# Top-p attention on one core: eight strip segments and four rounds in the second step, with another estimate of the band's end

## The reference, cut to what matters

```python
def _top_p_attention(X, W1, W2, W3):
    q = X @ W1.T @ W2.T
    k = X @ W3.T
    probs = jax.nn.softmax(q @ k.T / TAU, axis=-1)          # 2048 x 2048
    idx = jnp.argsort(-probs, axis=-1)
    sp = jnp.take_along_axis(probs, idx, axis=-1)
    cs = jnp.cumsum(sp, axis=-1)
    keep_sorted = cs - sp < TOP_P                           # TOP_P = 0.9
    mask = jnp.zeros(probs.shape, dtype=bool).at[rows, idx].set(keep_sorted)
    A = probs * mask
    return A / jnp.maximum(A.sum(-1, keepdims=True), 1e-12)
...
for n in range(STEPS):                                      # STEPS = 2
    A = _top_p_attention(Xa, W1, W2, W3)
    Xf = R @ Xf
    Xa = A @ Xa
    Z = Z + Xf @ U1[n].T + Xa @ U2[n].T
```

## Time and profile before

| | |
|---|---|
| median of 3 runs | 858.69 us (857.1 to 860.33) |
| the profiled execution | 859.55 us, span 857.8 us |
| PE, DVE, ACT, POOL busy | 85%, 73%, 53%, 32% of the span |
| the second step's groups, 495.4 to 784.2 us | DVE busy 274.8 of 288.8 us, ACT 185.0, POOL 126.3 |
| HBM | 57 GB/s over the span |

### The profile page before, as it was taken

One profiled execution on the slowest core, in us unless ns is written; L12 is line 12 of the kernel. 1 busy time (PEld: TensorE's weight loads), 2 busy tenths in 40 slices (PEclk: granted clock), 3 DMA queues, 4 the chain that ended last, 5 costly groups with the idle time before them and its releaser, 6 DMA issues.

```text
span 857.8 us, 15889 instructions
## 1 busy us (share of the span) xinstructions
PE 725.4 (85%) x5287; PEld 550.3 (64%) x5294; DVE 626.7 (73%) x2265; ACT 450.7 (53%) x689; POOL 273.9 (32%) x585
## 2 busy tenths in 40 slices
PE   4799999849999688999999997968678697798893
PEld 2566766529998444777777676755446585787463
DVE  6336656715444468998981799999899999999757
ACT  2366476115555145655653582849687585722153
POOL 4310422555666201112100152142250667770000
PEclk9899999879999899999999998879979898989897
DMA  9999730186887300000000000000000002001001
GB/s 155 193 173 156 136 72 16 40 213 192 231 235 205 118 1 1 1 1 2 2 2 1 1 2 2 2 1 2 0 1 1 2 2 74 26 3 32 1 2 49
DMA packets 82186, 50.37 MB, mean 59 GB/s; under 512 B 42193, under 2 KB 78929, under 8 KB 82097
## 3 DMA queue, kind: packets, MB, share of 16 engines
q1 hardware_dynamic: 64304, 28.35, 15.0%
q0 software_dynamic: 11456, 14.62, 9.1%
q10 hardware_dynamic: 6336, 6.32, 3.1%
HBM read 39.69 MB, written 9.57 MB: 57 GB/s over the span
## 4 chain that ended last, share of the span: by engine, by line
DVE 37%; PE 16%; ACT 5%; issue 5%; DVEq 1%; POOLq 1%; POOL 0%; ACTq 0%
DVE big L1602 6%; DVE cand L1366 5%; DVE cand L1520 4%; PE bank L2145 3%; PE bank L2049 3%; DVE hacc L1515 2%; DVE rm L1360 2%; DVE cand L1541 2%; DVE top L1536 2%; DVE big L1591 2%; PE bank L2128 2%; PE bank L2329 2%; DVE big L1588 2%; PE bank L2342 1%; ACT UT L1861 1%
## 5 line engine op out<-in xcount | busy, mean ns | idle before, releaser
L2128 PE MATMUL bank<-ident,big 128*128 128x128 f32 x512 | 79.6, 304 | 28.4 <-DVEq L1625 19.1
L2128 PEld LDWEIGHTS bank<-ident,big 128*128 128x128 f32 x512 | 61.2, 153 | 54.4 <-DVEq L1625 21.0
L1875 ACT ACTIVATE big<-bank 128x512 f32<-128x512 f32 x128 | 70.4, 597 | 46.6 <-PE bank L2128 46.6
L2049 PE MATMUL bank<-kk,qq 64*128 64x512 f32 x256 | 76.0, 711 | 16.8 <-ACT big L1845 16.2
L2056 PEld LDWEIGHTS bank<-parts,adjT 128*128 128x128 bf16 x1536 | 86.9, 98 | 3.2 <-issue 2.8
L2056 PE MATMUL bank<-parts,adjT 128*128 128x128 bf16 x1536 | 88.2, 219 | 0.1
L1845 ACT ACTIVATE big<-bank,negm 128x2048 f32<-128x2048 f32 x32 | 62.7, 1958 | 48.7 <-DVE fsc L1652 38.4
L1602 DVE SCALAR_TENSOR_TENSOR big<-big,st 128x2048 f32<-128x2048 f32 x32 | 73.9, 2348 | 2.9 <-PE bank L2128 2.9
L572 DVE TENSOR_TENSOR big<-big,adjT 128x1024 f32<-128x1024 f32 x32 | 39.8, 1249 | 48.5 <-ACT big L731 30.8
L428 POOL DMA_INDIRECT ys_scratch<-big,parts x62 | 59.9, 967 | 38.7 <-ACT big L774 28.6
L858 PEld LDWEIGHTS bank<-xrows,big 128*128 128x128 f32 x512 | 62.2, 196 | 14.6 <-DVE big L572 9.7
(11 more groups left out here) (373 smaller groups left out, 1448.1 us busy)
## 6 DMA issues: line engine op xcount, KB each, us to landing
big<-in_L_ffn_w_dram SPq DMA_DIRECT2D x93, 128.0 KB
big<-in_adj_dram POOLq DMA_DIRECT2D x8, 512.0 KB, 9.1
big<-xs_scratch ACTq DMA_DIRECT2D x31, 132.0 KB
kk<-in_adj_dram POOLq DMA_DIRECT2D x4, 512.0 KB, 11.3
qq<-in_adj_dram POOLq DMA_DIRECT2D x4, 512.0 KB, 15.0
xs_scratch<-hacc SPq DMA_DIRECT2D x9, 132.0 KB
xs_scratch<-hacc ACTq DMA_DIRECT2D x8, 132.0 KB
res<-in_x_dram SPq DMA_DIRECT2D x4, 256.0 KB, 5.0
```

Source lines behind the costliest of these rows:

```text
L1875: nc.scalar.activation(MT[:, 4 * q:4 * q + 4, s * P:(s + 1) * P], bank[:, 5 + q % 2, :].rearrange("p (j i) -> p j i", j=4), ACT.Copy).then ...
L2049: nc.tensor.matmul(bank[:, c, :], qq[lo:lo + DA, (g * G + s) * P:(g * G + s + 1) * P], kk[lo:lo + DA, c * CH:(c + 1) * CH], start=True, st ...
L2128: mm = nc.tensor.transpose(bank[:, 5 + q % 2, j * P:(j + 1) * P], mk[:, s, jt * P:(jt + 1) * P], ident[:, :])
```

## The change

Only the second step of the second graph layer changes.

- Each row tile's candidates come from 8 segments of 256 columns instead of 16 of 128. A segment is no longer one run of columns: it is four strips of 64 columns that stand 256 columns apart, all in one half of the row.
- Four rounds instead of five, on 64 candidates instead of 128; the 32 largest values below the band's end are used instead of 40. The short operations behind the rounds get shorter with it.
- `after_first` and `after_second` use another formula with a term that goes like the reciprocal of the count of values above the threshold. `after_first` has 12 operations instead of 8, with four drains as before; `after_second` has 11 as before, with five drains instead of six.

```diff
-        NSEG = (8, 16)
-        ROUNDS = (4, 5)
+        NSEG = 8
+        ROUNDS = 4
+        STRIPS = 4
...
-        SLOPE = 0.7
-        REACH = 40.0
+        JUMP = (1.23, 9.05, 0.476)
+        STEP = (1.0 / 0.823, 32.84, 38.66, 1.663)
...
                         nc.gpsimd.tensor_scalar(B(B_Y, s), B(B_S1, s), float(N), 0.5 * 2.0 ** FIRST, ALU.add, ALU.mult)
+                        nc.gpsimd.tensor_scalar(B(B_C, s), B(B_S1, s), -0.5, 0.5 * N + JUMP[2], ALU.mult, ALU.add)
...
                     nc.gpsimd.tensor_tensor(B(B_B, s), B(B_Y, s), B(B_R1, s), ALU.subtract)
-                    nc.gpsimd.tensor_scalar(B(B_TG, s), BI(B_TG, s), 1.0 / SLOPE, None, ALU.mult)
+                    nc.gpsimd.tensor_scalar(BI(B_C, s), BI(B_C, s), -1.0, 2.0 * ONE, ALU.mult, ALU.add)
+                    nc.gpsimd.tensor_scalar(B(B_TG, s), BI(B_TG, s), 1.0, None, ALU.mult)
                     pool.drain()
-                    nc.gpsimd.tensor_scalar(B(B_U, s), BI(B_B, s), -1.0 / SLOPE, ONE + FIRST * OCTAVE, ALU.mult, ALU.add)
+                    nc.gpsimd.tensor_scalar(B(B_U, s), BI(B_B, s), -1.0, B(B_TG, s), ALU.mult, ALU.add)
+                    nc.gpsimd.tensor_scalar(B(B_C, s), B(B_C, s), JUMP[1], JUMP[0], ALU.mult, ALU.add)
+                    nc.gpsimd.tensor_scalar(B(B_W, s), B(B_TG, s), STEP[0], None, ALU.mult)
                     pool.drain()
-                    nc.gpsimd.tensor_tensor(B(B_U, s), B(B_U, s), B(B_TG, s), ALU.add)
+                    nc.gpsimd.tensor_scalar(B(B_U, s), B(B_U, s), B(B_C, s), ONE + FIRST * OCTAVE, ALU.mult, ALU.add)
                     pool.drain()
...
-                    R8 = 8 * ROUNDS[n]
-                    SEG = N // NSEG[n]
-                    cg = cand1 if n else cand[:, b, :, :]
+                    R8 = 8 * ROUNDS
+                    cg = cand[:, b, :, :]
...
-                            for j in range(NSEG[n]):
-                                vc = op(nc.vector.max(cg[:, s, 8 * j:8 * j + 8], lowg[:, j * SEG:(j + 1) * SEG]))
+                            strips = lowg.rearrange("p (h a j n) -> p h j a n", h=2, a=STRIPS, j=NSEG // 2)
+                            for j in range(NSEG):
+                                vc = op(nc.vector.max(cg[:, s, 8 * j:8 * j + 8],
+                                                      strips[:, j // (NSEG // 2), j % (NSEG // 2), :, :]))
...
-                    for r in range(ROUNDS[n]):
+                    for r in range(ROUNDS):
...
-                            w = op(nc.vector.tensor_scalar(cand2[:, s, 0:64], cg[:, s, 64:128], S1(V_, s), None,
+                            w = op(nc.vector.tensor_scalar(cand2[:, s, 0:32], cg[:, s, 32:64], S1(V_, s), None,
                                                            ALU.is_equal, ALU.add, accum_out=S1(MH, s)))
```

More of the change, by code:

```diff
@@ L1044, in tries @@
             return 4 + 8 * (g - 1) + 2 * (2 * k + s) if g else 2 * s + k
-        tv = sb("tv", [P, G, 8 * max(ROUNDS)])
+        tv = sb("tv", [P, G, 8 * ROUNDS])
         cand = sb("cand", [P, 2, G, 64])
-        cand1 = cand[:, :, :, :].rearrange("p b s n -> p (b s n)").rearrange("p (s n) -> p s n", s=G)
-        top = sb("top", [P, G, 8 * max(ROUNDS)])
-        cum = sb("cum", [P, G, 8 * max(ROUNDS)])
+        top = sb("top", [P, G, 8 * ROUNDS])
+        cum = sb("cum", [P, G, 8 * ROUNDS])
         rm8 = sb("rm8", [P, 8])
@@ L1055, in build @@
         (T_, TB, F_, GE, Q_, FH, V_, SM, LO, HI, THETA, EX, EM, MH, DH) = range(15)
-        bt = sb("bt", [P, 13, G])
-        (B_R1, B_S1, B_R2, B_S2, B_T2, B_TB, B_TB1, B_TG, B_Y, B_B, B_C, B_U, B_V) = range(13)
+        bt = sb("bt", [P, 14, G])
+        (B_R1, B_S1, B_R2, B_S2, B_T2, B_TB, B_TB1, B_TG, B_Y, B_B, B_C, B_U, B_V, B_W) = range(14)
         first = sb("first", [P, 1])
@@ L1061, in build @@
         iota8 = sb("iota8", [P, 8])
-        cand2 = sb("cand2", [P, G, 128])
+        cand2 = sb("cand2", [P, G, 64])
         fsc = sb("fsc", [P, 2, G])
@@ L1220, in after_second @@
                     if g:
-                        nc.gpsimd.tensor_scalar(B(B_C, s), B(B_S2, s), float(N), 0.5, ALU.add, ALU.mult)
+                        nc.gpsimd.tensor_scalar(B(B_Y, s), B(B_S2, s), float(N), 0.5, ALU.add, ALU.mult)
+                        nc.gpsimd.tensor_scalar(B(B_C, s), B(B_S2, s), -0.5, 0.5 * N + STEP[3], ALU.mult, ALU.add)
                     else:
                         pool.wait_ge(counted, 2 * s + 2)
-                        nc.gpsimd.tensor_scalar(B(B_C, s), B(B_S2, s), 1.0, None, ALU.mult)
@@ L1225, in after_second @@
-                    nc.gpsimd.tensor_tensor(B(B_TG, s), B(B_TG, s), B(B_V, s), ALU.add)
+                        nc.gpsimd.tensor_scalar(B(B_Y, s), B(B_S2, s), 1.0, None, ALU.mult)
+                        nc.gpsimd.tensor_scalar(B(B_C, s), B(B_S2, s), -1.0, N + STEP[3], ALU.mult, ALU.add)
+                    nc.gpsimd.tensor_tensor(B(B_TG, s), B(B_W, s), B(B_V, s), ALU.add)
                     pool.drain()
-                    nc.gpsimd.tensor_tensor(B(B_Y, s), B(B_C, s), B(B_T2, s), ALU.mult)
@@ L1228, in after_second @@
-                    nc.gpsimd.tensor_scalar(B(B_C, s), B(B_C, s), -1.0, N + 0.5, ALU.mult, ALU.add)
+                    nc.gpsimd.tensor_tensor(B(B_Y, s), B(B_Y, s), B(B_T2, s), ALU.mult)
+                    nc.gpsimd.tensor_scalar(BI(B_C, s), BI(B_C, s), -1.0, 2.0 * ONE, ALU.mult, ALU.add)
                     pool.drain()
                     nc.gpsimd.tensor_tensor(B(B_B, s), B(B_Y, s), B(B_R2, s), ALU.subtract)
-                    nc.gpsimd.tensor_scalar(BI(B_C, s), BI(B_C, s), -1.0, 2.0 * ONE, ALU.mult, ALU.add)
+                    nc.gpsimd.tensor_scalar(B(B_W, s), B(B_C, s), STEP[2] * OCTAVE, STEP[1] * OCTAVE, ALU.mult, ALU.add)
@@ L1232, in after_second @@
                     pool.drain()
-                    nc.gpsimd.tensor_scalar(B(B_U, s), BI(B_B, s), -1.0 / SLOPE, None, ALU.mult)
-                    nc.gpsimd.tensor_scalar(B(B_C, s), B(B_C, s), REACH * OCTAVE, None, ALU.mult)
+                    nc.gpsimd.tensor_scalar(B(B_U, s), BI(B_B, s), -STEP[0], B(B_TG, s), ALU.mult, ALU.add)
+                    nc.gpsimd.tensor_tensor(B(B_W, s), B(B_W, s), B(B_C, s), ALU.mult)
                     pool.drain()
-                    nc.gpsimd.tensor_tensor(B(B_TG, s), B(B_TG, s), B(B_C, s), ALU.add)
@@ L1237, in after_second @@
-                    pool.drain()
-                    nc.gpsimd.tensor_tensor(B(B_U, s), B(B_U, s), B(B_TG, s), ALU.add)
+                    nc.gpsimd.tensor_tensor(B(B_U, s), B(B_U, s), B(B_W, s), ALU.add)
                     pool.drain()
@@ L1536, in group @@
                             got[s] = op(nc.vector.max(top[:, s, 8 * r:8 * r + 8], cand2[:, s, :] if n and r else cg[:, s, :]))
-                        if r + 1 < ROUNDS[n]:
+                        if r + 1 < ROUNDS:
                             for s in range(G):
```

1 line of the change is left out of this document (added).

## The result

The changed kernel takes 850.48 us (median of 20 runs, 847.06 to 858.1) against 860.11 us of the kernel before in the same comparison (20 runs): a ratio of 0.9901, 95% interval 0.9881 to 0.9921. It is faster by 1.0%, where 1.5% was forecast. The profiled executions show 847.06 us (span 845.3, mean clock 0.944) after 859.55 us. That difference, 12.5 us, flatters the change: 2.7 us of it arose before the second step began (g0 starts at 492.67 instead of 495.40) and 1.5 us behind its last group. A second profiled execution, 850.45 us, begins g0 at 495.85 and repeats all group lengths of the second step to 0.4 us.

The account below looks back on a forecast made before the run. It took VectorE to bound six groups, ScalarE and TensorE g2 and g3. Terms 8.4 + 2.4 + 2.4 + 0.9 + 0 - 1.1 = 13.0 us off 859.55 gave 846.5, as a median 845.7 us; range 839 to 852.

Parts of the forecast that it names:

- What VectorE saves: Second step, each group: segments 0.90, rounds 1.81 and shorter small operations 0.1 us, 2.8 us in all.
- g0 and g1: First two groups of the second step: 2.4 us gained in each, the rest of VectorE's saving turning into waits.
- the hold: g2: VectorE's earlier mask passes hold two GpSimd operations of after_first, so ScalarE gets its threshold 2.0 us late.
- I can't tell which, and take half: g2: a shorter TensorE pause might keep the upper clock and save 1.8 us; half counted, so g2 costs 1.1 us.
- VectorE's 2.8 us become a longer wait at the flags: g3, led by ScalarE and TensorE: VectorE's saving only lengthens its wait, so 0 us gained.
- g4, g5 and g6: all: These three groups get VectorE's whole saving, 3 x 2.8 = 8.4 us.
- The longer `after_first` in other groups delays ScalarE by at most two passes, 4.5 us, less than its spare time: 0: Groups other than g2: ScalarE's spare time covers the delay from GpSimd's longer chain, so it costs 0 us.
- TensorE has no pause from the start of the group to there: g7: TensorE works without pause through its filling matmuls, so VectorE waits for it and only 0.9 us is gained.
- No flag went up: Second step: the estimate still fits every row; the rival, a flag starting `exact`, meant 1030 us or more, chance 0.05.
- strips cost nothing: Segments: strip reads from SBUF add nothing; the rival, 2.7 us lost in four groups, meant 856 us, chance 0.05.
- GpSimd's hold spreads (850 us): Rival: a double hold in g3 and late band ends in g5 to g7 cost 4.5 us; chance 0.14.
- More arrives: Rival, 839 us: clock stays up in g2 and g7, g2 not held, g3 gains about 2 us; chance 0.10.

Follow-up runs that it names:

- after: The changed kernel's profiled execution: 847.06 us; its timed median is 850.48 us, ratio 0.9901 to the kernel before.
- after_again: The changed kernel run once more, unchanged, against the kernel before: ratio 0.9906.
- one_input: Changed kernel, second step's mask pass with one SBUF input (mask 0 and 1, no bisection there, result not the reference's): 0.9805 of the kernel before.
- interleave: Changed kernel with each row tile's mask pass right behind its own MATCH_REPLACE: not told apart from the changed kernel (group of runs 0.9869 to 0.9908).
- less_fill: Changed kernel with 7 instead of 20 filling matmuls ahead of the last flag_sum in g7: 0.9890 of the kernel before.
- inter_late: Changed kernel with the edits of interleave and late together: not told apart from the changed kernel (group of runs 0.9869 to 0.9908).
- before: The kernel without the change, profiled execution: 859.55 us; timed median 860.11 us in the comparison.
- rounds_only: Changed kernel with 16 segments of 128 columns kept, so only the new band end and four rounds: 0.9936 of the kernel before.
- late: Changed kernel with two after_first results ScalarE doesn't need computed behind its release: not told apart from the changed kernel (group of runs 0.9869 to 0.9908).
- late_max: Changed kernel with the edits of late and max_first together: not told apart from the changed kernel (group of runs 0.9869 to 0.9908).
- est_only: Kernel before with the new band end alone (longer after_first on GpSimd), segments and rounds as before: no difference measured.
- before_one_input: Kernel before with the one-SBUF-input mask pass and no bisection in the second step: 0.9966 of the kernel before.
- max_first: Changed kernel with row_max of group g+2 ahead of the mask passes: not told apart from the changed kernel (group of runs 0.9869 to 0.9908).
- max_less: Changed kernel with the edits of max_first and less_fill together: 0.9878 of the kernel before.

## Why the prediction was right and where it was wrong

The time came within the range of 839 to 852 us, but not within the 843 to 849 us that the sum was for, and it owes that to luck. By the traces 8.3 of the forecast 13.0 us came, and 3.3 of these are g3's, for which 0 was forecast; without them the time would be about 854 us (850.5 + 3.3, an estimate), above the range.

**What VectorE saves: right.** 2.8 us a group by the sum, 2.8 to 2.9 us in the busy time of g1 to g3.

**g0 and g1: right**, 2.9 and 2.1 us for 2.4 each.

**g2: the hold right, the clock wrong.** "I can't tell which, and take half" assumed that a shorter pause might keep TensorE's upper level. In after the pause for VectorE's mask shrank, and the logits ran at the lower level again, in order of time:

```profile
563.27 1.97 PE L2134 MATMUL bank<-ident,big 128*128 128x128 f32 x8 [3.46 <-DVEq L1631]
566.17 3.76 PE L2055 MATMUL bank<-kk,qq 64*128 64x512 f32 x8 [0.93 <-ACT big L1851]
```

3.76 us, after 3.46 us of waiting (3.78 after 1.80 + 3.70 in the earlier trace rows). The half of 1.8 us did not come: 1.6 us lost instead of 1.1.

**g3: 0 forecast, 3.3 us gained.** The step "VectorE's 2.8 us become a longer wait at the flags" kept ScalarE's and TensorE's own length of the group. That length is not fixed: TensorE ran g3 at 0.95 of its clock instead of 0.86 and was busy for 24.2 us instead of 26.8. Over the fourteen traces of this case g3's length goes with its clock: 33.2 to 33.7 us at 0.95 (after, after_again, one_input, interleave, less_fill), 35.2 at 0.90 (inter_late), 36.3 to 36.8 at 0.86 (before, rounds_only, late, late_max), 37.7 to 38.5 at 0.82 (est_only, before_one_input, max_first, max_less). late and late_max have the whole saving on VectorE and the clock of before, and with it 36.27 and 36.62 us against 36.76. So at an equal clock the forecast's 0 was right to 0.5 us, and the 3.3 us are the clock's. They are no accident of one execution, since after_again and less_fill have them too.

**g4 to g6: 8.4 us forecast, 2.8 came.** This is the step that failed: "g4, g5 and g6: all", and with it "The longer `after_first` in other groups delays ScalarE by at most two passes, 4.5 us, less than its spare time: 0". The delay is right, the spare time isn't. Three things took 5.6 us.

First, in g4 the logits came at the lower level (3.78 us; in before the same ones took 1.99 after the same pause), so `row_max` waited 1.04 us, and the group gained 1.6 us. In order of time, TensorE in before, TensorE in after, VectorE in after:

```profile
648.35 1.99 PE L2049 MATMUL bank<-kk,qq 64*128 64x512 f32 x8 [1.50 <-ACT big L1845]
```
```profile
638.90 3.78 PE L2055 MATMUL bank<-kk,qq 64*128 64x512 f32 x8 [1.50 <-ACT big L1851]
```
```profile
642.76 2.30 DVE L1365 MAX8 rm<-bank 128x8 f32<-128x2048 f32 x1 [1.04 <-PE bank L2055]
```

Second, the logits, late by 1.8 us, put ScalarE's sweeps, and so `after_first`, against the mask passes that come earlier. Two operations are held in g4. Then ScalarE and GpSimd start late in g5: GpSimd's norm ends only at 691.38, the first row tile's `after_first` stands behind it (691.47 to 695.08, none of it held) and lets ScalarE wait 4.55 us, and the second row tile's falls into the mask passes. g6 repeats it, with 3.31 us behind the norm and 3.38 us for two held operations. GpSimd and ScalarE, in order of time:

```profile
661.02 2.45 POOL L1216 TENSOR_SCALAR bt<-bt 128x1 f32<-128x1 f32 x1 [0.18 <-issue]
663.63 2.12 POOL L1218 TENSOR_SCALAR bt<-bt 128x1 f32<-128x1 f32 x1 [0.15 <-issue]
...
691.47 0.19 POOL L1200 TENSOR_SCALAR bt<-bt 128x1 f32<-128x1 f32 x1
...
694.89 0.19 POOL L1219 TENSOR_SCALAR bt<-bt 128x1 int32<-128x1 f32 x1
...
695.41 2.25 POOL L1201 TENSOR_SCALAR bt<-bt 128x1 f32<-128x1 f32 x1
697.72 2.23 POOL L1206 TENSOR_SCALAR bt<-Z 128x1 f32<-128x1 f32 x1
```
```profile
666.11 2.00 ACT L1867 ACTIVATE UT<-big,bt 128x2048 int8<-128x2048 f32 x1 [3.56 <-POOL bt L1219]
...
695.17 2.00 ACT L1867 ACTIVATE UT<-big,bt 128x2048 int8<-128x2048 f32 x1 [4.55 <-POOL bt L1219]
702.89 2.00 ACT L1867 ACTIVATE UT<-big,bt 128x2048 int8<-128x2048 f32 x1 [3.50 <-POOL bt L1219]
...
738.65 2.00 ACT L1867 ACTIVATE UT<-big,bt 128x2048 int8<-128x2048 f32 x1 [3.38 <-POOL bt L1219]
```

One wait is within ScalarE's spare time; a row of them is not, since each begins with what the last left. It surfaces at `row_max` of g6, 1.72 us for logits.

Third, VectorE's own small operations between the scan and MATCH_REPLACE now meet GpSimd's norm. In g5 of after, VectorE, then GpSimd:

```profile
687.89 0.46 DVE L1578 SCALAR_TENSOR_TENSOR tv<-top,st,cum 128x32 f32<-128x32 f32 x1
...
688.61 0.96 DVE L1585 TENSOR_SCALAR eq<-iota,st 128x8 f32<-128x8 f32 x2
...
689.67 0.91 DVE L1590 TENSOR_SCALAR eq<-iota,st 128x8 f32<-128x8 f32 x2
```
```profile
687.84 1.70 POOL L1281 TENSOR_TENSOR xnT<-xnT,lng 128x128 f32<-128x128 f32 x4
689.69 1.69 POOL L1284 TENSOR_TENSOR res<-res,xnT 128x128 f32<-128x128 f32 x4
```

Each of the two pairs took 0.48 us before, where the norm had ended (at 699.4) before the pairs began (at 702.07). About 1.1 us in g5 (0.48 + 0.43 + 0.2) and 0.8 us in g6 went this way, and with the waits of 0.2 and of 1.7 us (and 0.3 of issue) they make up what the two groups lack, to 0.3 us.

one_input says how much of the 5.6 us is the hold's. Without it g4 to g6 take 99.0 us, 3.9 less than in after, of which 0.8 us is the shorter time behind the flags: about 3 us (an estimate). The other 2.6 us stayed there too: g4's `row_max` waited 1.0 us for logits, and the small operations met the norm.

**g7: 0.9 us forecast, 1.3 us lost.** That VectorE would wait for the filling matmuls was right, the size was not. For the kernel before it was so, but in after "TensorE has no pause from the start of the group to there" no longer held. Since ScalarE's last sweep of g6 was late by 3.38 us, its copies for g7 began late, TensorE paused, and the filling ended late. TensorE of after, in order of time:

```profile
743.41 5.12 PE L2134 MATMUL bank<-ident,big 128*128 128x128 f32 x24 [2.26 <-ACT big L1881]
...
767.38 4.26 PE L311 MATMUL bank<-adjT,identb 128*128 128x512 bf16 x19
```

767.38 + 4.26 = 771.64, which is 32.05 us behind the start of the group; before it was 781.45 - 751.84 = 29.6. The wait at the flags became 2.97 us instead of 1.9, and two band passes at the group's start waited 0.76 + 0.29 us for GpSimd. In one_input, without the hold, the flags waited 1.66 us and g7 was 31.04 us, 1.4 us shorter than before: this is the forecast's case.

**No flag went up, strips cost nothing: right.**

**The rivals.** "GpSimd's hold spreads (850 us)", given 0.14, has the right time and is right that the hold spreads, but not along its two paths: g3 had no hold, and late band ends cost VectorE only 0.76 + 0.29 us. It looked at what VectorE needs from GpSimd a group later; what mattered is the second threshold, which ScalarE needs within the group. The price of the hold, about 7 us of the eight groups by one_input, is above its 4.5; that its time came out all the same is g3's clock. "More arrives" had the gain in g3 right (about 2 forecast, 3.3 came); the clock in g2 did not stay up and g2 was held, and its 839 us were neared only by the kernel without the hold (842.29).

What stays open: why TensorE's level falls in one group and not in the next at equal pauses, and so whether g3's gain would outlast another edit. Nor was a mask pass tried that has one SBUF input and still writes the kept values; one_input writes 0 and 1.

## What to carry to other kernels

When VectorE is made faster, what it meets on the engines beside it moves too. So work out anew where the other engines' short chains fall against its long two-input passes, for every group and not only for the one already at the limit. A pass with two SBUF inputs costs its own time and also stops each short GpSimd chain that falls into it; here a pass with one input, in a kernel that doesn't compute the result and has no bisection, was worth about as much again (1.0%) as the whole change, a third of it also without the change. Laying the chains anew with the pass as it is shortened the waits in all four tries, but none was measurably faster than the changed kernel. And a filling matmul sized for the old gap turns into the wait once the gap closes.

## What the hardware showed that was not expected

- The hold goes with the form of the pass and not with its length: passes of 2.34 us with one SBUF input and with two, GpSimd's operations of one column in them 0.19 to 0.26 and 2.12 to 2.45 us. It is counted as busy time, not as a wait.
- It works in the other direction too: pairs of 128x8 TENSOR_SCALAR with two per-partition scalars took 0.91 to 0.97 instead of 0.48 us beside GpSimd's 128x128 operations, while a TENSOR_SCALAR_CACHE_REDUCE of 128x32 with one scalar just ahead of them stayed at 0.24. The two forms differ in the scalars, in the accumulator and in the columns; no run separates these.
- MAX8 over four strips of 64 columns in SBUF ran at the pace of 256 columns in one run in PSUM: 0.328 and 0.331 us from start to start.
- The logits ran at 1.99 or 3.78 us after the same pause of 1.50 us.
